# Projecting step two's queries and keys inside step one's loop, and reordering the first loads, in a two-step top-p graph attention kernel

## What is computed

```python
for n in range(2):                      # STEPS
    q = Xa @ W1.T @ W2.T                # (N, 64)
    k = Xa @ W3.T                       # (N, 64)
    probs = softmax(q @ k.T)
    A = keep the largest probs of a row until their sum reaches 0.9; renormalize
    Xf = R @ Xf                         # R: adjacency + I, rows normalized
    Xa = A @ Xa
    Z = Z + Xf @ U1[n].T + Xa @ U2[n].T
```

## Time and profile before

| | |
|---|---|
| median of 3 runs | 2792.64 us (2786.88 to 2792.99) |
| the profiled execution, its own time | 2795.35 us |
| its span, first to last instruction | 2793.6 us |
| mean granted TensorE clock | 0.932 |
| TensorE matmuls busy | 2358.4 us, 84% |
| VectorE busy | 2201.9 us, 79% |
| ScalarE busy | 1071.5 us, 38% |
| GpSimd busy | 140.9 us, 5% |
| instructions | 53551 |

### The profile page before, as it was taken

The page is one execution under the profiler, slowest core; times in us unless marked ns, Lnnn a source line. Parts: engine busy times, 40 slices in busy tenths (PEclk is TensorE's granted clock), DMA queues, the critical chain, the costliest instruction groups (busy, mean ns, idle before and its releaser), DMA issues. The chain is left out here.

```text
span 2793.6 us, 53551 instructions
## 1 busy us (share of the span) xinstructions
PE 2358.4 (84%) x17759; PEld 1987.9 (71%) x17759; DVE 2201.9 (79%) x6636; ACT 1071.5 (38%) x1785; POOL 140.9 (5%) x353
## 2 busy tenths in 40 slices
PE   5899998767888997887886649996999999999985
PEld 1566666445677776776775539995999999999952
DVE  3777777288887889888789867775999999999846
ACT  4566666432333333332333040003434344443423
POOL 0000000101111111000000010000000000000000
PEclk9999999988898998998997869998999999999997
DMA  3000000020222221222220234543333333333320
GB/s 127 2 2 1 1 1 2 1 99 11 90 100 100 99 100 50 100 99 100 99 99 2 99 127 175 217 171 126 111 115 133 116 130 118 129 120 126 99 87 25
DMA packets 57106, 245.00 MB, mean 88 GB/s; under 512 B 6705, under 2 KB 18352, under 8 KB 43120
## 3 DMA queue, kind: packets, MB, share of 16 engines
q1 hardware_dynamic: 56816, 241.94, 24.7%
HBM read 235.10 MB, written 6.82 MB: 87 GB/s over the span
## 5 line engine op out<-in xcount | busy, mean ns | idle before, releaser
L1933 PE MATMUL a_acc<-H,pT 128*128 128x128 f32 x4056 | 548.0, 277 | 11.1 <-ACT a_rows L1965 3.8
L1933 PEld LDWEIGHTS a_acc<-H,pT 128*128 128x128 f32 x4056 | 495.4, 192 | 28.1 <-DVE pT L2067 19.3
L71 DVE MAX8 cand<-e 128x8 f32<-128x64 f32 (+3 forms) x1898 | 302.6, 239 | 129.4 <-issue 129.2
L935 PE MATMUL small<-XR,wT 128*128 128x128 f32 x2756 | 377.2, 283 | 28.8 <-ACT wT L1132 28.1
L819 PE MATMUL lg<-kT,qs 128*128 128x512 f32 (+1 forms) x742 | 350.8, 612 | 47.1 <-ACT e L1076 34.9
L935 PEld LDWEIGHTS small<-XR,wT 128*128 128x128 f32 x2756 | 343.1, 197 | 45.1 <-ACT wT L1132 45.1
L2067 DVE TENSOR_TENSOR pT<-a_tr,a_adjT 128x512 f32<-128x512 f32 (+1 forms) x546 | 316.6, 645 | 22.3 <-PE a_tr L1892 19.2
L839 PE MATMUL accR<-XR,adj 128*128 128x129 f32 x2704 | 322.8, 281 | 0.0
L1892 PE MATMUL a_tr<-ident,prob 128*128 128x128 f32 x2028 | 311.9, 274 | 10.9 <-ACTq L1959 10.9
L839 PEld LDWEIGHTS accR<-XR,adj 128*128 128x128 f32 x2704 | 319.5, 198 | 0.0
L1132 ACT ACTIVATE wT<-tr 128x512 f32<-128x512 f32 (+1 forms) x371 | 206.0, 566 | 268.3 <-PE tr L925 266.4
(11 more groups left out here) (334 smaller groups left out, 2456.6 us busy)
## 6 DMA issues: line engine op xcount, KB each, us to landing
adj<-in_adjT SPq DMA_DIRECT2D x52, 1664.0 KB, 7.2
g_adj<-in_adjT SPq DMA_DIRECT2D x26, 1664.0 KB, 6.9
a_adj<-in_adj SPq DMA_DIRECT2D x26, 1664.0 KB, 6.8
a_adjT<-in_adjT SPq DMA_DIRECT2D x156, 256.0 KB, 3.9
a_adjT<-in_adjT SPq DMA_DIRECT2D x26, 128.0 KB, 4.2
XT<-in_x_t SPq DMA_DIRECT2D x1, 1664.0 KB, 13.5
hT_scratch<-hT SPq DMA_DIRECT2D x1, 1664.0 KB, 12.1
nsT_scratch<-nsT SPq DMA_DIRECT2D x1, 1664.0 KB, 6.2
```

Source lines behind the costliest of these rows:

```text
L71: eng.max(cand[:, n, :], src[:, n * seg:min((n + 1) * seg, width)])
L935: mm = eng.matmul(accA[:, :], wT[(k * NC + c - 1) % 2][:, o:o + P], xa[:, j, 0:P], start=(j == 0), stop=(j == T - 1))
L1933: mm = eng.matmul(acc[:, :], pT[g % RING][:, (j % 4) * P:(j % 4 + 1) * P], H[:, j, :], start=(j == 0), stop=(j == T - 1))
```

## The change

- The loads are issued as W3T twice (into both column halves of a wider tile), XT, then W1T, W2T twice, then XR[0], H, UT, UT, with three semaphores. TensorE waits for the first three before k, for the W1T and W2T loads before q, and for the rest only ahead of the first flags. GpSimd waits for the last four before it hands out any q.
- Step one's head: k for all chunks, h and q for chunk 0, the logits of pairs 0 and 1, then h and q for the other six chunks, then the flags of pair 0.
- In step one, `project_h` follows the update of each pair (256 columns), and `project_kq` of the pair before stands after the second attend part (256 columns each for k and q). ScalarE copies h behind zsA, k and q behind the second weight copy. Step two's k and q lie in rows 64 to 127 of kT and qT; logits run over 64 rows instead of 128, without zeros.
- The last pair of step one makes the first six chunks of both slots of step two's pair 0; the seventh follows at the head of step two, ahead of the grid. Step two's own projections and the copy of xT to XT are gone. VectorE takes the segment tops of the six chunks first, the rest after the seventh.
- The parity of the e buffers in step two is swapped throughout; h1 moves into XR[2], zsR into XT, and the ones column of XR[2] is set in step two. The zeroing of kT and qs is gone. kT stays 128 rows, qT becomes 128 rows.

The diff, cut, each part moved left:

```diff
-def segment_tops(eng, src, width, cand, seg):
-    for n in range(-(-width // seg)):
+def segment_tops(eng, src, width, cand, seg, begun=0):
+    for n in range(begun, -(-width // seg)):
...
-STEP_CH = PROJ + T * NC
+FIRST_PROJ = NC + 2
+WHOLE = NC - 1
...
-h1 = find.work[0:DA, 0:NP]
+h1 = XR[2][0:DA, :, :].rearrange("p a n -> p (a n)")[:, 0:NP]
+half_of = (slice(0, DA), slice(DA, 2 * DA))
...
-W2T = sb("W2T", [DA, DA])
-W3T = sb("W3T", [P, DA])
+W2T = sb("W2T", [DA, 2 * DA])
+W3T = sb("W3T", [P, 2 * DA])
...
-zsR, zsA = sb("zsR", [P, 2, P]), sb("zsA", [P, 2, P])
+zsR, zsA = XT[:, 13 * P:15 * P].rearrange("p (a n) -> p a n", a=2), sb("zsA", [P, 2, P])
...
+next_h = XT[0:DA, 11 * P:13 * P]
...
+def first_apart(eng, pair):
+    pair(0, 0, 3)
+    with eng.Fori(0, (PAIRS - 3) // 2) as pp:
+        pair(pp * 2 + 1, 1, 3)
+        pair(pp * 2 + 2, 0, 3)
+    for p in range(PAIRS - 2, PAIRS):
+        pair(p, p % 2, PAIRS - 1 - p)
...
 def chunk(step, p, slot, c):
-    return step * STEP_CH + PROJ + (p * 2 + slot) * NC + c
+    base = PROJ + step * T * NC
+    if step == 0 and (at(p, 0) or at(p, 1)):
+        base = FIRST_PROJ
+    if step == 1 and at(p, 0):
+        return base + (slot * WHOLE + c if c < WHOLE else 2 * WHOLE + slot)
+    return base + (p * 2 + slot) * NC + c
+def bank(step, p, slot, c):
+    return chunk(step, p if isinstance(p, int) else 2, slot, c) % 2
...
-eng.dma_start(XR[0][:, :, 0:P], d["x_rows"]).then_inc(loaded, 16)
-eng.dma_start(H[:, :, :], d["x_rows"]).then_inc(loaded, 16)
-eng.dma_start(XT[:, :], d["x_t"]).then_inc(loaded, 16)
-eng.dma_start(W1T[:, :], d["W1T"]).then_inc(loaded, 16)
-eng.dma_start(W2T[:, :], d["W2T"]).then_inc(loaded, 16)
-eng.dma_start(W3T[:, :], d["W3T"]).then_inc(loaded, 16)
-eng.dma_start(UT[:, 0, :, :], d["U1T"]).then_inc(loaded, 16)
-eng.dma_start(UT[:, 1, :, :], d["U2T"]).then_inc(loaded, 16)
+for h in half_of:
+    eng.dma_start(W3T[:, h], d["W3T"]).then_inc(xt_loaded, 16)
+eng.dma_start(XT[:, :], d["x_t"]).then_inc(xt_loaded, 16)
+eng.dma_start(W1T[:, :], d["W1T"]).then_inc(in_loaded, 16)
+for h in half_of:
+    eng.dma_start(W2T[:, h], d["W2T"]).then_inc(in_loaded, 16)
+eng.dma_start(XR[0][:, :, 0:P], d["x_rows"]).then_inc(rows_loaded, 16)
+eng.dma_start(H[:, :, :], d["x_rows"]).then_inc(rows_loaded, 16)
+eng.dma_start(UT[:, 0, :, :], d["U1T"]).then_inc(rows_loaded, 16)
+eng.dma_start(UT[:, 1, :, :], d["U2T"]).then_inc(rows_loaded, 16)
...
-eng.wait_ge(loaded, 16 * N_LOADS)
+eng.wait_ge(rows_loaded, 16 * 4)
 for step in range(2):
-    eng.wait_ge(lg_free, 2 + step * STEP_CH + PROJ)
+    def give_q_of(st, p, k):
+        eng.wait_ge(qs_free, seq(st, p, k) + 1)
+        eng.tensor_copy(qs[k][half_of[st], :], qT[half_of[st], bass.ds((p * 2 + k) * P, P)])
+        eng.drain()
+        eng.sem_inc(qs_ready, 1)
     def give_q(p, k):
-        eng.wait_ge(qs_free, seq(step, p, k) + 1)
-        eng.tensor_copy(qs[k][0:DA, :], qT[:, bass.ds((p * 2 + k) * P, P)])
-        eng.drain()
-        eng.sem_inc(qs_ready, 1)
+        give_q_of(step, p, k)
...
+if at(p, PAIRS - 1):
+    eng.wait_ge(kq_copied, 1)
+    give_q_of(1, 0, 0)
+    give_q_of(1, 0, 1)
...
-if step == 1:
+if step == 0:
+    eng.wait_ge(lg_free, 2 + FIRST_PROJ)
+    for p in range(2):
+        give_q(p, 0)
+        give_q(p, 1)
+    eng.wait_ge(lg_free, 2 + chunk(0, 2, 0, 0))
+else:
     make_grid()
-for p in range(2):
-    give_q(p, 0)
-    give_q(p, 1)
+    eng.wait_ge(kq_copied, PAIRS)
+    give_q(1, 0)
+    give_q(1, 1)
...
-def project(which, lhsT, rhs, c):
-    n = step * STEP_CH + which * NC + c
+def project(n, lhsT, rhs):
     eng.wait_ge(lg_free, n + 1)
     eng.matmul(lg[n % 2][0:DA, 0:rhs.shape[1]], lhsT, rhs, start=True, stop=True)\
        .then_inc(lg_ready, 1)
-def logit(p, k, c):
+def logit_of(st, p, k, c):
     if c == 0 and at(p, PAIRS):
         eng.wait_ge(taken_q_ready, 1)
     elif c == 0:
-        eng.wait_ge(qs_ready, seq(step, p, k) + 1)
-    bank = chunk(step, 0, k, c) % 2
+        eng.wait_ge(qs_ready, seq(st, p, k) + 1)
     sl = cols(c, N)
-    eng.wait_ge(lg_free, chunk(step, p, k, c) + 1)
-    eng.matmul(lg[bank][:, 0:sl.stop - sl.start], qs[k][:, :], kT[:, sl],
-               start=True, stop=True).then_inc(lg_ready, 1)
+    eng.wait_ge(lg_free, chunk(st, p, k, c) + 1)
+    eng.matmul(lg[bank(st, p, k, c)][:, 0:sl.stop - sl.start], qs[k][half_of[st], :],
+               kT[half_of[st], sl], start=True, stop=True).then_inc(lg_ready, 1)
     if c == NC - 1:
...
+def next_logit(p, k, c):
+    if not at(p, PAIRS - 1):
+        logit_of(0, p + 2, k, c)
+    elif c < WHOLE:
+        logit_of(1, 0, k, c)
...
-    mm.then_inc(zA_ready, 1)
+    if step == 1:
+        mm.then_inc(zA_ready, 1)
+def project_h(p):
+    eng.matmul(xz[0:DA, 0:2, :].rearrange("p a n -> p (a n)"), W1T[:, :],
+               xT[:, :, :].rearrange("p a n -> p (a n)"), start=True, stop=True).then_inc(zA_ready, 1)
+def project_kq(p):
+    eng.wait_ge(zsA_ready, turn_of(step, p) + 2)
+    eng.wait_ge(h_copied, p + 1)
+    eng.matmul(xz[:, 2:4, :].rearrange("p a n -> p (a n)"), W3T[:, :],
+               xT[:, :, :].rearrange("p a n -> p (a n)"), start=True, stop=True)
+    eng.matmul(xz[:, 0:2, :].rearrange("p a n -> p (a n)"), W2T[:, :], next_h,
+               start=True, stop=True).then_inc(kq_made, 1)
 def pair(p, b, rest):
+    ahead = rest >= 2 or at(p, PAIRS - 1)
     for c in range(NC - 2):
         attend_part(p, b, 0, c)
-    if rest >= 2:
-        logit(p + 2, 0, 0)
-        logit(p + 2, 0, 1)
+        if c == 1 and not at(p, 0):
+            project_kq(p - 1)
+    if at(p, PAIRS - 1):
+        eng.wait_ge(kq_copied, p)
+    if ahead:
+        next_logit(p, 0, 0)
+        next_logit(p, 0, 1)
     for c in range(NC - 2, NC + 1):
         attend_part(p, b, 0, c)
     attend_part(p, b, 1, 0)
     for c in range(1, NC - 1):
         attend_part(p, b, 1, c)
-        if rest >= 2 and c + 1 < NC:
-            logit(p + 2, 0, c + 1)
+        if ahead and c + 1 < NC:
+            next_logit(p, 0, c + 1)
     for c in range(NC - 1, NC + 1):
         attend_part(p, b, 1, c)
-    if rest >= 2:
-        logit(p + 2, 1, 0)
+    if ahead:
+        next_logit(p, 1, 0)
     if rest:
         turn_flags(p + 1)
-    if rest >= 2:
+    if ahead:
         for c in range(1, NC):
-            logit(p + 2, 1, c)
+            next_logit(p, 1, c)
+    if not at(p, 0):
+        eng.wait_ge(kq_copied, p)
     turn_attended(p)
     update(p)
+    project_h(p)
...
-eng.wait_ge(addedA, step * PAIRS)
-for c in range(NC):
-    project(0, W1T[:, :], XT[:, cols(c)], c)
-for c in range(NC):
-    eng.wait_ge(lg_free, 2 + step * STEP_CH + c + 1)
-    project(1, W2T[:, :], h1[:, cols(c)], c)
-for c in range(NC):
-    project(2, W3T[:, :], XT[:, cols(c)], c)
-eng.wait_ge(lg_free, 2 + step * STEP_CH + PROJ)
-for p in range(2):
-    logits(p, 0)
-    logits(p, 1)
-    if step == 1 and p == 0:
-        make_grid()
+if step == 0:
+    eng.wait_ge(xt_loaded, 16 * 3)
+    for c in range(NC):
+        project(c, W3T[:, 0:DA], XT[:, cols(c)])
+    eng.wait_ge(in_loaded, 16 * 3)
+    project(NC, W1T[:, :], XT[:, cols(0)])
+    eng.wait_ge(lg_free, 2 + NC + 1)
+    project(NC + 1, W2T[:, 0:DA], h1[:, cols(0)])
+    eng.wait_ge(lg_free, 2 + FIRST_PROJ)
+    for p in range(2):
+        logits(p, 0)
+        logits(p, 1)
+    for c in range(1, NC):
+        project(chunk(0, 1, 1, NC - 1) + c, W1T[:, :], XT[:, cols(c)])
+    for c in range(1, NC):
+        eng.wait_ge(lg_free, 2 + chunk(0, 1, 1, NC - 1) + c + 1)
+        project(chunk(0, 1, 1, NC - 1) + NC - 1 + c, W2T[:, 0:DA], h1[:, cols(c)])
+    eng.wait_ge(consts, 1)
+    eng.wait_ge(zeroed, 1)
+    eng.wait_ge(rows_loaded, 16 * 4)
+else:
+    eng.wait_ge(kq_copied, PAIRS)
+    logit(0, 0, NC - 1)
+    logit(0, 1, NC - 1)
+    make_grid()
+    logits(1, 0)
+    logits(1, 1)
+    eng.wait_ge(addedA, PAIRS)
 if step == 0:
     turn_flags(0)
-    over_pairs(eng, pair, tail=3)
+    first_apart(eng, pair)
+    project_kq(PAIRS - 1)
...
+def copy_next_logit(p, b, k, c):
+    if not at(p, PAIRS - 1):
+        copy_logit_of(0, p + 2, b, k, c)
+    elif c < WHOLE:
+        copy_logit_of(1, 0, 1, k, c)
+def copy_h(p):
+    eng.activation(next_h, xz[0:DA, 0:2, :].rearrange("p a n -> p (a n)"), ACT.Copy)\
+       .then_inc(h_copied, 1)
+def copy_kq(p):
+    own = bass.ds(p * 2 * P, 2 * P)
+    eng.wait_ge(kq_made, p + 1)
+    eng.activation(kT[half_of[1], own], xz[half_of[1], 2:4, :].rearrange("p a n -> p (a n)"),
+                   ACT.Copy)
+    eng.activation(qT[half_of[1], own], xz[half_of[1], 0:2, :].rearrange("p a n -> p (a n)"),
+                   ACT.Copy).then_inc(kq_copied, 1)
...
 def pair(p, b, rest):
+    ahead = rest >= 2 or at(p, PAIRS - 1)
     for c in range(NC - 2):
         copy_weights(p, 0, c)
+        if c == 1 and not at(p, 0):
+            copy_kq(p - 1)
     if rest:
         exps(p + 1, 1 - b, 0)
...
             exp_tops(p + 1)
         if c == NC - 1:
             copy_row(p, b, 1)
```

(105 more changed lines are left out.)

32 lines of the change are left out of this document (12 added, 20 removed).

## The result

| | before | after |
|---|---|---|
| median of the runs | 2792.81 us (2786.88 to 2795.08, 4 runs) | 2857.82 us (2851.89 to 2861.51, 4 runs) |
| span of the profiled execution | 2793.6 us | 2856.8 us |
| mean granted TensorE clock | 0.932 | 0.902 |
| TensorE busy | 2358.4 us, 84% | 2461.7 us, 86% |
| VectorE busy | 2201.9 us | 2199.9 us |

The account below looks back on a forecast made before the run. It took TensorE's instruction stream, plus a few hand-overs with ScalarE, to bound the loop. Start -8.8, loop +17.6 and passage -23.7 gave -14.9 us: 2792.6 to about 2778, range 2768 to 2790; the rest was to shift as a block.

Parts of the forecast that it names:

- the loop's part: Step one's loop: three more matmuls and copies a pair cost +17.6 us in all, bounds 14 to 23.
- The debit for the clock at the start: Start, around 17 to 21 us: TensorE works by fits and starts, so first logits run slower; 1.0 us, bounds 0 and 2.5.
- Loads: Start: X transposed, issued at about 1.9 behind two 32 KB loads, lands 7.2 us later, at about 9.0.
- Rival (A): Start: loads advance side by side, X transposed still lands at about 19.3; total 2786.5, no difference; chance 0.10.
- First logit: Start: first logits begin at 21.3 instead of 41.74 us, q being held by the rows, H and U loads until 20.8.
- Transposes of the loop: End of the start: the loop's first transposes come at about 77 to 78 us; start gain 8.8 us.
- Loop: Step one's loop: 1.6 us more a pair, 36.5 us a pair, over eleven pairs +17.6 us.
- The cover of the two kq copies: Loop: the copies fall where ScalarE idles 1.20 us and TensorE has 0.9 us of products; cost nothing, uncovered 0.7.
- (B): Loop: projections don't hide their weight loads, 2.7 us a pair in all; total -2.8, 2789.8 us; chance 0.12.
- (C): Loop: kq becomes a serial exchange of TensorE and ScalarE, about 4.0 us a pair; total +11.5, 2804 us; chance 0.09.
- Passage: Last pair's start to step two's first tops: 48.1 us plus hand-overs instead of 72.4; -23.7 us, bounds -19 and -26.
- the start's part: Loads and first projections: logits 20.4 us earlier, twelve deferred chunks cost 10.6, clock debit 1.0; -8.8 us.

Follow-up runs that it names:

- e1_full_rows: The changed kernel with its logit matmuls over 128 rows again, zeros in the unused halves: 2779.09 us, ratio 0.9955 to the kernel before.
- e9_old_load_order: e1_full_rows with pair 0's flags ahead of the twelve deferred projection chunks, and loads issued in the order of the kernel before: 2780.55 us, ratio 0.9952.

## Why the prediction was wrong

**The step that failed** is one sentence of the loop's part: "K=64 instead of 128 rows changes nothing: the W2T chunks have 64 rows and run at the pace of the others." The row is right and was read for more than it shows. Its chunks came behind seven 128-row chunks, with the clock up and 0.30 us of idle between. Of a 64-row stream that starts with the clock down, and of one between 128-row matmuls, the trace of before shows nothing, and the logits of pair 1 and all of step two were about to become such streams. In place of "nothing" the runs show 78.7 us between 64 and 128 rows, and 2.2% for that edit alone. The debit for the clock at the start was set at 1.0 within bounds of 0 and 2.5, from 128-row rows; the flags alone came 16.9 later than with full rows (89.50 and 72.64). Nor had the prediction a term for the changes between 128-row and 64-row matmuls in the loop, 1.3 us a pair.

The Trainium skill, "TensorE: Matmul & The Clock Gate", section "Why this matters for your kernels", says that a single matmul of 32 rows takes as long as one of 128. The runs, with 64 rows, agree at the full clock (6.09 and 6.11 us for seven chunks). Behind a wait they don't (11.07 and 7.71), since the clock comes back in one stream and not in the other; there the measurement decides.

**With 128-row logits the rest nearly held.** e1_full_rows is the change as forecast: 2779 against 2778. That the two lie 1 us apart is in part luck: 14.9 us were forecast and 11.7 measured, and the kernel before had a median 1.8 lower in that call. Stage by stage:

- **Loads.** X transposed landed 7.2 us after its issue at 1.67, at 8.7 to 8.9, forecast 9.0. The prediction's estimate of up to 1.4 us more, from the Trainium skill ("DMA: Bandwidth & Descriptors", section Bandwidth), was not borne out; the figure there is for loads issued by GpSimd, and these go by the sync engine. Rival (A) is out by this landing, and by e9_old_load_order, where the old order brings X transposed back to 19.8.
- **First logit.** 22.3, forecast 21.3: the last load released GpSimd at 21.79 in the changed kernel, not 20.8, and the first seven chunks took 7.71.
- **Transposes of the loop.** 78.66, forecast 77 to 78; 7.9 us earlier than before against 8.8.
- **Loop.** 36.89 a pair, forecast 36.5. The new matmuls start at these places (e1_full_rows, a pair end):

```profile
115.16 0.71 PE L999 MATMUL xz<-UT,xT 128*128 128x128 f32 x4 [0.47 <-ACT xT L1247]
115.80 0.65 PE L1005 MATMUL xz<-xT,W1T 128*64 128x256 f32 x2
118.71 0.60 PE L1012 MATMUL xz<-xT,W3T 128*128 128x256 f32 x2
119.24 0.70 PE L1014 MATMUL xz<-XT,W2T 64*128 64x256 f32 x2
```

- The h matmul starts the first product 0.72 later than in the earlier trace rows (2.56 us behind the update's start instead of 1.84), forecast 0.75. The kq matmuls cost 1.2, forecast 0.87. One part of that is in the sum: 6.11 us was divided by seven, but the seventh chunk has half the columns, so 512 columns are 0.94 and kq is 0.94 too. The others are that starts and ends are not overlapped as in a stream, and that the W2T matmul has 64 rows between matmuls of 128. A pair costs 1.93 more instead of 1.6, and the loop, from the first transposes to the last pair's start, 20.6 (438.34 against 417.74) instead of 17.6. The cover of the two kq copies on ScalarE held, and rivals (B) and (C) did not come about: TensorE waits no longer than in the earlier trace rows, and a pair costs 1.93 more, where they have 2.7 and 4.0. (The terms given for (C) add up to 4.5 and not 4.0; it is out either way.)
- **Passage.** From 517.00 to the end of the tops at 565.17, 48.2 us, forecast 48.7: 32.3 up to the transposes of the attended rows, where 33.7 was taken, and 15.8 for the tail, where the sum had 14.4 and 0.6 for hand-overs. It gave 24.2 against 23.7.
- **Sum.** -7.9 + 20.6 - 24.2 = -11.5, forecast -14.9; the medians of that call differ by 11.7. The rest, from the tops to the end, is 2207.6 long in this one execution and 2216.9 in that of before, a difference that the medians don't show: this execution (2774.60) is the fastest of its seven runs, that of before (2795.35) stands 2.5 above its median.

Rival (C) was the only slower case, at 0.09. No rival had the clock, although the start's part already named it: the trace showed 7.71 against 6.11 after a wait, and the change altered the very shape that has to bring the clock back. That the forecast missed is no bad luck: it had no term for this.

**Was the idea worth anything?** Yes, by little: with full rows it is 11.7 us faster. Load order gives 9.4 us (e9), the passage 24 against 21 paid in the loop; flags first, an edit on top of the change, 8 at the tops of step two (10 in the medians). The height of one operand spent all that the change won and 65 us more.
